# Graph network, two layers on one core: the first edge stage fetches 8 of its 391 tiles of rows through SP

## The reference

```python
def _L0_gnn_ref(features, src, dst, edge_weight, W1, W2, b1, b2):
    messages = features[src] * edge_weight[:, None]
    aggregated = jax.ops.segment_sum(messages, dst, num_segments=N_NODES)
    act = lambda x: jax.nn.leaky_relu(x, negative_slope=LEAKY_ALPHA)
    out = act(features * aggregated @ W1 + b1) + act(aggregated @ W2 + b2)
    sq = jnp.sum(out * out, axis=1, keepdims=True)
    return out * jax.lax.rsqrt(jnp.maximum(sq, L2_EPS))
...
x = _layernorm(x + _L0_gnn_ref(x, src, dst, edge_weight, ...), axis=-1)
x = _layernorm(x + _L1_gnn_ref(x, edge_index, edge_weight, ...), axis=-1)
```

## Time and profile before

| what | value |
|---|---|
| median of three runs | 2966.61 us |
| the profiled execution | 2967.57 us |
| its span, first to last instruction | 2965.8 us |
| POOL busy | 2349.5 us (79%) |
| DVE busy | 2216.3 us (75%) |
| PE busy | 2141.6 us (72%) |
| gathers of the first stage, L246 | 391, 974 ns each |
| scatters of the first stage, L259 | 391, 1592 ns each |
| first instruction of the second stage on POOL | 1264.94 us |

### The profile page before, as it was taken

How to read it: one execution, slowest core, us unless ns; L and a number is a source line. 1 busy time by engine, 2 the same in 40 slices (tenths; PEclk the granted TensorE clock), 3 DMA queues, 4 the chain that set the end, 5 groups by cost and what they waited for, 6 DMA issues and landing times. The chain is left out here.

```text
span 2965.8 us, 39231 instructions
## 1 busy us (share of the span) xinstructions
PE 2141.6 (72%) x11956; PEld 1669.1 (56%) x11956; DVE 2216.3 (75%) x5628; ACT 1071.0 (36%) x1964; POOL 2349.5 (79%) x1770
## 2 busy tenths in 40 slices
PE   3035555555555553369999989899999889799997
PEld 3035555454554543347777766666666666566664
DVE  5079888888888885557788777677777767288888
ACT  0000000000000000035555545455555445388887
POOL 7777888888888888758887888888888887488888
PEclk8555555555555555579999999999999989799998
DMA  9998888888888776567787777777777776366664
GB/s 229 208 204 186 177 174 185 171 184 181 180 178 172 157 143 137 98 177 181 186 184 184 178 162 177 157 177 177 171 173 177 177 156 139 93 198 207 206 207 156
DMA packets 1035719, 516.28 MB, mean 174 GB/s; under 512 B 540224, under 2 KB 998000, under 8 KB 1035512
## 3 DMA queue, kind: packets, MB, share of 16 engines
q1 hardware_dynamic: 764616, 372.57, 47.8%
q0 software_dynamic: 143888, 76.97, 19.1%
q10 hardware_dynamic: 127008, 64.23, 7.6%
HBM read 269.84 MB, written 243.78 MB: 173 GB/s over the span
## 5 line engine op out<-in xcount | busy, mean ns | idle before, releaser
L303 PE MATMUL sums<-xg,weigh 128*128 128x64 f32 x1960 | 432.8, 417 | 524.2 <-ACT ms L326 372.4
L555 POOL DMA_INDIRECT state<-ms,sidx x391 | 635.1, 1624 | 148.6 <-issue 116.5
L303 PEld LDWEIGHTS sums<-xg,weigh 128*128 128x128 f32 x1960 | 418.6, 326 | 557.2 <-issue 492.4
L259 POOL DMA_INDIRECT table<-ms,sidx x391 | 622.3, 1592 | 136.4 <-issue 114.6
L371 DVE TENSOR_SCALAR weigh<-rowp,key,ew 128x128 f32<-128x128 f32 (+3 forms) x784 | 423.8, 602 | 170.7 <-PE rowp L291 163.5
L536 POOL DMA_INDIRECT box<-table,node_dst x391 | 388.2, 993 | 129.7 <-issue 107.3
L246 POOL DMA_INDIRECT xg<-in_x,node_src x391 | 380.7, 974 | 120.5 <-issue 105.8
L326 ACT ACTIVATE ms<-sums 128x256 f32<-128x256 f32 x98 | 37.5, 383 | 1148.6 <-DMA table<-ms,sidx 1038.4
L377 DVE SCALAR_TENSOR_TENSOR seen<-rowp,key,earlier 128x128 f32<-128x128 f32 (+3 forms) x784 | 383.0, 543 | 0.0
L587 PE MATMUL z_p<-turned_s,wz 128*128 128x512 f32 x588 | 339.1, 661 | 27.9 <-ACT turned_s L660 20.9
L597 PE MATMUL o_p<-cenz,leaky 128*128 128x65 f32 x2352 | 284.5, 278 | 29.7 <-DVE leaky L745 29.7
(11 more groups left out here) (95 smaller groups left out, 3462.2 us busy)
## 6 DMA issues: line engine op xcount, KB each, us to landing
box<-table SPq DMA_DIRECT2D x97, 768.0 KB, 5.3
joins<-weigh ACTq DMA_DIRECT2D x98, 640.0 KB, 3.8
weigh_in<-joins SPq DMA_DIRECT2D x98, 640.0 KB
table<-rows SPq DMA_DIRECT2D x97, 512.0 KB, 5.3
pair<-state SPq DMA_DIRECT2D x97, 512.0 KB, 3.8
xin<-in_x SPq DMA_DIRECT2D x97, 256.0 KB, 6.2
state<-y SPq DMA_DIRECT2D x97, 256.0 KB
out<-y SPq DMA_DIRECT2D x97, 256.0 KB, 2.2
```

What stands on the lines that cost most here:

```text
L259: pool.indirect_dma_start(out=table[:, :], out_offset=bass.IndirectOffsetOnAxis(ap=sidx[0][:, i:i + 1], axis=0), in_=ms[k % MR][:, b, :], ...
L303: last = pe.matmul(sums[k % 2][:, a * D:(a + 1) * D], block_of(0, k, b)[:, a * P:(a + 1) * P], xg[:, k * WT + b, :], start=b == a, stop=b ...
L555: pool.indirect_dma_start(out=state[:, :], out_offset=bass.IndirectOffsetOnAxis(ap=sidx[1][:, at:at + 1], axis=0), in_=ms[k % SM][:, b, :] ...
```

## The change

Windows 94 and 95 (`PICKED`, 8 tiles) are no longer gathered by POOL. SP fetches their rows: for each of the 128 partitions, `pick(p)` reads the eight row numbers of that partition from `node_src` into registers of SP and issues eight transfers of one row (256 bytes), whose source address comes from the register, without a check of the bounds. The picks stand in SP's rounds 0 to 89, after the load of the round, 128/90 partitions a round on average, which is 11.4 rows. POOL gathers the other 96 windows (`LISTED`, 383 tiles) in their order; `arrival` and `upto` count in that list, and `upto` reaches its end at k = 92, before at 95. `join` of windows 94 and 95 waits for the semaphores `picked`. SP waits for the indices (`loaded`) before the weights are loaded.

```diff
+    PICKED = range(NWIN - 4, NWIN - 2)
+    LISTED = [w for w in range(NWIN) if w not in PICKED]
+    GATHERED = FILLED - len(PICKED) * WT
...
-                    of = min(2, NWIN - COARSE - 2 * pair)
-                    missing = MISSING if COARSE + 2 * pair + of == NWIN else 0
+                    of = min(2, len(LISTED) - COARSE - 2 * pair)
+                    missing = MISSING if COARSE + 2 * pair + of == len(LISTED) else 0
...
+                picked = [sem(f"picked0_{q}") for q in range(len(PICKED))]
...
+                        def pick(p):
+
+                            tiles = slice(PICKED[0] * WT, (PICKED[-1] + 1) * WT)
+                            _, rows = nc.values_load_multi_w_load_instructions(
+                                node[0][p:p + 1, tiles], engines=(mybir.EngineType.SP,), min_val=0, max_val=N - 1,
+                                skip_runtime_bounds_check_because="src lists rows of x, which the reference gathers unchecked")
+                            for b, row in enumerate(rows):
+                                sp.dma_start(xg[p:p + 1, tiles.start + b, :], x[bass.ds(row, 1), :]).then_inc(picked[b // WT], 16)
...
+                        sp.wait_ge(loaded, 16 * (1 + (ER > 0)))
                         for to, of in weight_loads:
...
                             if c0 + XR < NCH:
                                 load_x(c0 + XR)
+                            for p in range(min(P * c0 // (NCH - 8), P), min(P * (c0 + 1) // (NCH - 8), P)):
+                                pick(p)
...
-                        def gather(i):
+                        def gather(j):
+                            i = LISTED[j // WT] * WT + j % WT
...
-                                                    ).then_inc(gathered[arrival(i // WT)[0]], 16)
+                                                    ).then_inc(gathered[arrival(j // WT)[0]], 16)
...
-                            return min(EARLY + (TILES - EARLY) * k // (NWIN - 3), FILLED)
+                            return min(EARLY + (GATHERED + MISSING - EARLY) * k // (NWIN - 6), GATHERED)
...
-                            q, landed = arrival(k)
-                            pe.wait_ge(gathered[q], landed)
+                            if k in PICKED:
+                                pe.wait_ge(picked[k - PICKED[0]], 16 * WT * P)
+                            else:
+                                q, landed = arrival(LISTED.index(k))
+                                pe.wait_ge(gathered[q], landed)
```

## The result

The changed kernel takes 2970.86 us (median of 14 runs) where the kernel before takes 2965.85 (14 runs): ratio 1.0018, 95% interval 1.0011 to 1.0025. That 2970.86 lies inside the range, 2953 to 3070 us, is luck: the range reached up that far for rival (a), which did not come.

A forecast was written before the change was run, and what follows sets the result against it. The prediction took POOL's gathers and scatters to bound the first stage. Tail -5.2, early waits -1 and SP's picks 0 gave -6 us, from 2967.57 to 2961 us; range 2953 to 3070.

The forecast's parts named there:

- rival (a): SP's round becomes the bound once a picked row costs SP over 0.78 us; 3095 us at 0.91; chance 0.30.
- Parts 1 to 3: POOL, end of first stage: eight gathers leave (10.3 us), after scatter 92 starts; 6.1 us return as landing waits; gain 5.15.
- the tail: First stage from scatter 92's start to the last scatter's end: 52.66 us against 57.81, a gain of 5.15 us.
- Part 4: SP's rounds: 1024 one-row transfers, 11.4 a round, fit in SP's free time of 8.84 us a round.
- X: SP's time per picked row: forecast 0.59 us, between 0.32 and 2.5, with 0.78 available.
- hidden, at cost 0: SP busy 9.3 of 11.40 us a round with the picks, so they add nothing to the time.
- Early waits: POOL's waits from 154 to 300 us, 10.6 us in all: picks spreading SP's burst gain 1 us, at most 9.
- Packets: DMA rings: the picks bring about as many data packets as the gathers had, 1024.
- Rival (c): Small transfers slow scatter landings, eating 5 us over 90 rounds: 2967 us; chance 0.60 shared with the forecast.
- The sum: Whole kernel: -5.2 us tail, -1 early waits, 0 for SP, so -6 us from 2967.57 to 2961.

## Why the prediction was wrong

- **Parts 1 to 3** (which gathers leave, the tail, 5.15 us) hold: 4.5 us in the changed kernel's trace, 4.6 in that with the rows left out, whose median is 3.6 us under the runs of before beside it.
- **Part 4, the size of X.** I took 0.59 us, it is 0.73. Transfer and register work together were right, 0.46 us against 0.32 + 0.13. Eight registers are one reading, as assumed, but it takes 1.94 us in the median and not 1.1: 0.24 a row, not 0.14. The rest are steps between instructions. At 0.73 us, X stayed just under the 0.78 at which SP would have been the bound. The two figures that the prediction weighed hold in part. The Trainium skill (Runtime: NRT & Kernel Launch, "Instruction fetch mechanics") has about 200 ns per register; here it is 0.26 us a register right behind a load of x and 0.10 right behind another pick, so no one figure fits. The Trainium skill (DMA: Bandwidth & Descriptors, "Latency and other measured facts") has a floor of about 600 ns; the least reading of eight registers took 757 ns, that of four 557, and it is paid once for all of them.
- **Part 4, "hidden, at cost 0": the step that failed.** SP did keep its pace (82.5 us of waiting for ACT left, though in 17 rounds and not, as I wrote, in every one), and rival (a) did not come. But I asked only whether SP had the time, and not what its issues would then be beside. The store and load start later in POOL's window, and the clearing, which stands behind the picks, moves from 0.4 us after the window's first scatter to anywhere in it. Where its packets fill the DMA engines just when the last scatter's are due, POOL waits. In place of 0, the stage lost 18.6 us between windows 13 and 92, 14.8 of them in gaps behind a clearing. The diff showed the picks ahead of the clearing, and I counted the clearing as time of SP alone.
- **Early waits.** I took 1 us of gain, the changed kernel had 5.6. With the rows left out there was none, and with the clearing before the picks there was none either (-1.1). So the spreading of SP's first rounds by picks doesn't explain it alone; the cause stays open.
- **Packets.** I wrote that the picks bring about as many data packets as the gathers had. The trace has 1024 packets of 256 bytes for the picks, where a gather is 16 packets of 2 KB, so 128 for the eight.
- **Rival (c)** had the right place, late landings, and the wrong cause, the small transfers. Windows 73 to 86 rule out that the transfers do it by themselves: they have picks and no clearing, and no late gap. That they add to what a clearing does is not ruled out: with small clearings the picks still lose some 5 us.
- **The sum** is then -4.5 (tail) - 5.6 (early) + 18.6 = +8.5 us at the last scatter (1270.8 against 1262.3); the profiled spans differ by 4.4 us and the medians by 5.0. What is left between 8.5 and 4.4 lies in the two later stages, which the change doesn't touch; why they are shorter in that profile is not worked out.

Left open: the 2.3 us behind windows 53 and 61 and the 0.9 behind window 90, what picks add to a clearing, and by what rule the packets of the scatters wait: for 4 us none passes in one kernel, and some do in the kernel before. The kernel with the clearing before the picks shows that place is not easily held while SP is nearly full.

## What to carry to other kernels

Free time on the issuing engine is not enough to call an added step hidden: write down every transfer that stands behind it, and where in the critical engine's cycle each will now fall. A large background transfer is best cut so small that it can't hold back a landing that someone waits for; here that alone was worth 10 us. A wait put down to an engine whose own wait ends at the same landing is a wait for the landing.

## What the runs showed of the hardware that was not expected

- The same 1 MB transfer costs POOL 0.2 us when issued 0.4 us after the window's first scatter and 1.84 us at 5.6 us.
- While the packets of a 1 MB clearing were out, none of POOL's queue started for 4 us (3317 packets of SP's queue, 94.7% of the DMA engines' time, in the kernel with the clearing after the second scatter).
- Reading eight registers from on-chip memory took SP between 0.76 and 2.96 us in the changed kernel, and it depends on what SP issued just before: 2.08 us in the median behind a load of x (90 readings), 0.80 behind another pick (38). For four registers, with half the picks, it was 1.27 and 0.59.
